# DLRM tower on one Trainium2 core: the sums of two units in one run on TensorE, with a new table of places for the side work

## The reference

```python
e = jnp.stack([tbl_0[ids[:, 0]], ..., tbl_39[ids[:, 39]]], axis=1)   # [512, 40, 32]
iidx, jidx = jnp.triu_indices(40, k=1)
z = jnp.einsum('bpd,pde,bpe->bp', e[:, iidx, :], bilinear_matrices, e[:, jidx, :])   # [512, 780]
h = jnp.concatenate([z, dense_ctx], axis=1)          # [512, 796]
h = jnp.maximum(h @ W_top1 + b_top1, 0.0)            # 796 -> 512
h = jnp.maximum(h @ W_top2 + b_top2, 0.0)            # 512 -> 256
y = h @ W_top3                                       # 256 -> 1
```

## Time and profile before

| | |
|---|---|
| median of 3 runs | 208.48 us (206.97 to 209.49) |
| the profiled execution | 208.05 us, of which the span from first to last instruction 206.0 us |
| TensorE matmul busy | 186.4 us (90% of the span) |
| VectorE busy | 165.7 us (80%) |
| GpSimd busy | 97.7 us (47%) |
| ScalarE busy | 14.7 us (7%) |
| granted TensorE clock, mean | 0.992 |

### The profile page before, as it was taken

The page is one execution under the profiler, slowest core; times in us unless marked ns, Lnnn a source line. Parts: engine busy times, 40 slices in busy tenths (PEclk is TensorE's granted clock), DMA queues, the critical chain, the costliest instruction groups (busy, mean ns, idle before and its releaser), DMA issues.

```text
span 206.0 us, 3187 instructions
## 1 busy us (share of the span) xinstructions
PE 186.4 (90%) x1368; PEld 58.0 (28%) x1368; DVE 165.7 (80%) x168; ACT 14.7 (7%) x23; POOL 97.7 (47%) x101
## 2 busy tenths in 40 slices
PE   0077969999599999999999999999999999999995
PEld 0033313422233432223222222222322222223443
DVE  0399999999999999999987777878989888892500
ACT  2001000010000010100101011101100001001313
POOL 0478777777787777777777777700000000000000
PEclk9999978999999999999999999999999999999999
DMA  5999991001000000010010000000000000000000
GB/s 109 358 402 402 419 397 42 13 16 16 12 14 13 13 13 13 13 18 14 13 16 13 13 13 13 17 5 0 0 5 0 0 0 3 0 0 0 0 0 0
DMA packets 7949, 12.39 MB, mean 60 GB/s; under 512 B 3040, under 2 KB 6000, under 8 KB 7808
## 3 DMA queue, kind: packets, MB, share of 16 engines
q1 hardware_dynamic: 4432, 10.52, 13.7%
q0 software_dynamic: 3072, 1.58, 4.7%
q10 hardware_dynamic: 432, 0.10, 0.3%
HBM read 12.19 MB, written 0.00 MB: 59 GB/s over the span
## 4 chain that ended last, share of the span: by engine, by line
PE 84%; DVE 10%; DMA 4%; issue 1%; SPq 0%; ACT 0%; DVEq 0%
PE y_ps L421 31%; PE z_ps L444 25%; PE t_ps L403 10%; PE t_ps L391 9%; DVE hot L325 4%; DMA table<-hot_tables 4%; PE y_ps L458 3%; DVE low L337 3%; DVE rest L335 3%; PE y_ps L375 2%; PE y_ps L452 2%; PE t_ps L467 1%; DVE prod L357 1%; PE z_ps L436 0%; SPq L254 0%
## 5 line engine op out<-in xcount | busy, mean ns | idle before, releaser
L357 DVE TENSOR_TENSOR prod<-y_ps,xt 128x1024 f32<-128x1024 f32 x110 | 122.2, 1166 | 13.8 <-PE y_ps L421 11.3
L244 POOL DMA_INDIRECT x_rows<-rows,row x96 | 96.7, 1007 | 29.2 <-issue 29.0
L421 PE MATMUL y_ps<-xt,m_sb 32*128 32x512 f32 x420 | 71.0, 649 | 0.0
L444 PE MATMUL z_ps<-prod,sel 128*32 128x512 f32 x420 | 58.3, 604 | 0.0
L421 PEld LDWEIGHTS y_ps<-xt,m_sb 32*128 32x128 f32 x420 | 24.2, 185 | 40.5 <-issue 29.2
L325 DVE TENSOR_SCALAR hot<-hot_id,number 128x2048 bf16<-128x2048 int16 x36 | 25.8, 761 | 8.0 <-DMA hot_id<-hot_ids 7.5
L391 PE MATMUL t_ps<-hot,table 128*32 128x512 bf16 x144 | 15.8, 410 | 17.5 <-DVE low L337 17.5
L403 PE MATMUL t_ps<-z_t,w_sb 128*128 128x512 f32 x40 | 22.2, 642 | 0.0
L444 PEld LDWEIGHTS z_ps<-prod,sel 128*32 128x32 f32 x420 | 8.7, 108 | 41.6 <-issue 27.2
L391 PE MATMUL t_ps<-hot,rest 128*32 128x512 bf16 x144 | 15.6, 406 | 0.0
L391 PE MATMUL t_ps<-hot,low 128*32 128x512 bf16 x144 | 15.5, 402 | 0.0
(11 more groups left out here) (20 smaller groups left out, 32.0 us busy)
## 6 DMA issues: line engine op xcount, KB each, us to landing
hot_id<-hot_ids SPq DMA_DIRECT2D x4, 512.0 KB, 7.2
w_sb<-w SPq DMA_DIRECT2D x1, 1792.0 KB, 18.6
x_rows<-rows,row POOLq DMA_INDIRECT x96, 2.4
table<-hot_tables SPq DMA_DIRECT2D x2, 640.0 KB, 10.6
table<-hot_tables SPq DMA_DIRECT2D x2, 512.0 KB, 8.2
m_sb<-mats SPq DMA_DIRECT2D x1, 640.0 KB
m_sb<-mats SPq DMA_DIRECT2D x1, 576.0 KB
m_sb<-mats SPq DMA_DIRECT2D x1, 512.0 KB
```

The costliest lines, as they stand in the source:

```text
L244: pool.indirect_dma_start(out=x_rows[:, g, c, :], out_offset=None, in_=rows, in_offset=bass.IndirectOffsetOnAxis(ap=row[:, n:n + 1], axis= ...
L357: nc.vector.tensor_tensor(prod[:, k % PROD_UNITS, 2 * half:2 * half + w, :], y_ps[:, 2 * slot:2 * slot + w, :], xt[:, t, :].unsqueeze(1).t ...
L421: last = nc.tensor.matmul(y_ps[:, 2 * slot + s % 2, :], m_sb[rows, k, :], xt[rows, u, :], start=True, stop=True)
L444: last = nc.tensor.matmul(z_ps[s * DIM:(s + 1) * DIM, :], window, prod[:, k % PROD_UNITS, s, :], start=starts, stop=(k >= last_unit(b) - 1 ...
```

## The change: one run of sums behind every second unit

`schedule()` keeps a counter `summed`. Behind the tiles of an odd unit k it now writes all sums that are due by `LAG`, which are two units' (k - 3 and k - 2); behind the tiles of an even unit it writes none. The copy of a block stands behind its last sum as before. The table `AFTER` is another one: which rounds, l1 matmuls and turns stand behind (or ahead of) which unit. Nothing is computed differently, and no instruction is added or taken away. What `AFTER` lists for an even k now stands between the tiles of the two units of a pair, what it lists for an odd k behind the run of sums.

```diff
 AFTER = {
-    "hot": [-1, -1, -1, -1, -1, -1, -1, -1, -1, -1, -1, -1, -1, -1, -1, -1, 0, 1, 1, 1, 1, 2, 2, 3, 3, 3, 7, 7, 8, 8,
-        9, 9, 10, 11, 12, 13],
-    "l1": [26, 27, 28, 29, 30, 31, 32, 33, 34, 35, 36, 37, 42, 44, 45, 46, 47, 47, 48, 49],
-    "turn": [3, 10, 21, 28, 36, 45],
+    "hot": [-1, -1, -1, -1, -1, -1, -1, -1, 0, 0, 0, 0, 0, 0, 1, 1, 1, 1, 2, 3, 3, 4, 4, 5, 6, 6, 6, 7, 7, 8, 8, 10,
+        11, 12, 12, 14],
+    "l1": [24, 26, 28, 30, 31, 32, 34, 36, 40, 42, 42, 43, 44, 44, 46, 47, 48, 50, 52, 52],
+    "turn": [3, 10, 19, 26, 32, 36],
 }
...
     steps = []
+    summed = 0
     for k in range(-1, UNITS + LAG):
         if 0 <= k < UNITS:
             steps.append(("unit", k))
-        if k >= LAG:
-            steps.append(("sum", k - LAG))
-            b, r = divmod(k - LAG, PER_BLOCK)
-            if k - LAG == last_unit(b):
-                steps.append(("z", b))
+
+        while summed <= k - LAG and (k % 2 == 1 or k >= UNITS):
+            steps.append(("sum", summed))
+            if summed == last_unit(summed // PER_BLOCK):
+                steps.append(("z", summed // PER_BLOCK))
+            summed += 1
         for what in ("hot", "l1"):
             steps += [(what, n) for n, after in enumerate(AFTER[what]) if after == k]
     return steps
```

## The result

| | before | changed |
|---|---|---|
| median | 207.87 us (206.97 to 209.49, 4 runs) | 214.28 us (212.41 to 215.04, 4 runs) |
| profiled execution | 208.05 us, span 206.0 | 214.34 us, span 212.5 |
| ratio | | 1.0286, 95% interval 1.019 to 1.0383 |

Slower by 2.9% where 212.6 us was forecast, and inside the range of 208.6 to 215.6. Beside a later pair of kernels the changed one was timed again: 212.54 us (212.14 to 212.87, 4 runs) against 208.05, ratio 1.0206 (1.015 to 1.0262). The forecast was 4.5 us above the kernel before, a ratio of 1.02; by the medians the first set lies 6.4 us above it and the second 4.5.

The account below looks back on a forecast made before the run. VectorE set the pace without side work, TensorE with l1 matmuls. Twenty pairs at 5.37 us plus l1, dense inputs and turn made 113.9 instead of 109.2 us; +4.5 us on 208.05 gave 212.6 us, range 208.6 to 215.6.

Parts of the forecast that it names:

- The loop: Pair's first product, waiting last half, two sums, next tiles: 2.34 + 1.86 + 1.17 = 5.37 us, against VectorE's 4.53.
- Side work between the tiles: One l1 matmul between a pair's tiles costs nothing, two there 0.54 us more; one behind the sums 1.06 more.
- Fewer changes of kind: On TensorE, joined runs save some 0.12 to 0.2 us per change of matmul kind; two sums take 1.86 us.
- rival B: Faster from unit 24 on through saved changes and cheaper l1 matmuls, without loop and turn: 204.2 us, chance 0.07.
- D's wait: The odd unit's second half waits for the product of the even unit's first half, three halves before it.
- The last turn: VectorE's turn, moved from unit 45 to 36, waits for GpSimd's 96th gather; unit 36 not before 136.6 us: 0.7 us.
- The start: Up to unit 14, first product at 75.7 us as before; loss 0, at most 1.3 us from slow TensorE near unit 2.
- sign of being wrong: Prediction wrong if pairs without l1 come at 4.6 us, or the first 75 us differ by more than 2 us.
- 0.55 lost and regained by unit 6: VectorE loses 0.55 us where unit 0's products come ahead of the second table's one-hots, regained by unit 6.
- Rival A: Loop overlapped, pairs without l1 at 4.53 us, but unit 36 still waits until 136.6: 210.2 us, chance 0.13.
- Rival C: Loop as forecast, plus 1.3 us of slow TensorE in the first 35 us and 1.0 of signal: 215 us, chance 0.13.
- 0.05 us of signal in each loop: In the worse case, 0.05 us more of signal in each of 20 loops, 1.0 us in all.

Follow-up runs that it names:

- Experiments 1 and 2: Changed kernel with l1 matmuls moved from between the tiles to behind the sums: 227.76 us; changed kernel with VectorE making an even unit's second product first: 248.84 us.
- the kernels with ten and with eight pairs: Kernel before, l1 matmuls joined between tiles and sums joined only in some pairs: ten, 206.86 us; eight, no l1 run crossing an output-tile change, 205.25 us.
- experiment 3: Changed kernel, but with single sums and the old one-hot places up to unit 13, pairs only from unit 14: 212.73 us, ratio 1.0233.

## Why the prediction was right, point by point

- **The loop, 5.37 us a pair.** Right: 5.35 to 5.37 in the pairs from unit 14 on that have no more than one l1 matmul between the tiles and no wait for a gather (5.41 or 5.42 in those of units 26 and 34), in five kernels. Experiments 1 and 2 lengthen it by an l1 matmul or a product and the pair follows; a count of TensorE's work or of its changes of kind does neither.
- **Side work between the tiles free, behind the sums 1.06, two in the middle 0.54 more.** Right: 5.36 with one in the middle, 6.42 with one behind. The pairs at 42, 44 and 52 with their extras take 6.96, 5.90 and 5.91 us (forecast: 6.97, 5.91 and 5.91), and the 20 pairs 113.2 us, whose sum was forecast at 113.2 without the turn.
- **Fewer changes of kind (rival B).** The saving is what the rows of before gave: two sums 1.86 us. The Trainium skill (TensorEngine Tiling (Array Packing), Tiling Modes) has every change of tiling mode drain TensorE, which speaks for joining. In the changed kernel the time saved reappears as D's wait (0.47 us of pause at 90.48). Only in the kernels with ten and with eight pairs, with the loop hidden, does it reach the end of the kernel.
- **The last turn, 0.7 us.** The mechanism was right and its size a little small: 1.1 us in experiment 3. In the changed kernel's first profile it cost nothing, because VectorE came late for another reason (next point); in its second it cost 0.8 us, the pair of units 34 and 35 taking 6.25 instead of 5.42. The turn there came 3.9 us behind the last gather's issue (132.70 to 136.56), not the 2.4 of the median DMA.
- **The start, 0 to 1.3 us.** This is the term that was mis-sized. Unit 14's first product started at 78.47 us, not at 75.7: 2.7 us, above the bound of 1.3 and above the 2 us that the prediction itself had named as a sign of being wrong. On two other runs with the same first 24 units it started at 76.2 and 76.3, 0.5 late. The windows show the granted clock (column 8) in the stretches 20 to 35 and 50 to 60, first in the changed kernel's first profile, then in its second; the last one is of experiment 3, which has the old start:

```profile
20.00:35.00 15.00, 12.11 (x140) 4.32 (x140) 13.92 (x16) 0.69 (x2) 11.65 (x12) 0.89 0.82 317
50.00:60.00 10.00, 7.48 (x74) 2.08 (x62) 9.97 (x11) 0.60 (x1) 7.86 (x8) 0.83 0.07 12
```

```profile
20.00:35.00 15.00, 10.84 (x150) 3.77 (x144) 14.95 (x18) 0.60 (x1) 11.65 (x12) 1.00 0.79 309
50.00:60.00 10.00, 9.08 (x90) 3.09 (x90) 9.19 (x10) 0.00 (x0) 7.87 (x8) 0.83 0.09 14
```

```profile
50.00:60.00 10.00, 7.36 (x75) 2.32 (x76) 9.97 (x11) 0.00 (x0) 7.86 (x8) 0.83 0.08 13
```

A slow stretch behind TensorE's pause of 2.5 or 2.6 us at 50 us comes in all three. (In the profile of the kernel before, a pause of 2.82 us ends at 53.82, and the clock stays at 1.00.) In experiment 3, with single sums there, it costs nothing: VectorE is busy 9.97 of the 10 us and reaches unit 14 at 75.64. In the changed kernel the tiles of unit 7 and two sums at the low clock lie ahead of unit 8's tiles, and VectorE waits 1.03 us at 61.13 in the first profile and 0.81 at 58.87 in the second. So the prediction had the right mechanism for its upper bound, a slow stretch that makes VectorE wait, but looked for it near unit 2 only. What the paired sums would cost at this place at the full clock no profile shows.

The other 1.3 us or so of the first profile come in the first 35 us. VectorE waits 1.5 us for one-hot rounds between 14 and 18 us, where it waited 0.5 before and 0.2 in the second profile: TensorE's matmuls reach their short duration at 17.1 us, instead of 15.2 and 14.2. And it waits 0.34 us under a low clock between 24 and 27 us, behind a pause of 1.91 us. The kernel before has such a stretch too (granted clock 0.89 from 20 to 35 us) and no wait of VectorE behind it. In both profiles of the changed kernel VectorE also idles 0.70 us ahead of unit 0's first product, which the prediction had as 0.55 lost and regained by unit 6; an idle 0.47 us that the kernel before has ahead of unit 6, at 47.60, is gone instead. That the slow stretches vary from run to run is why two medians of the same kernel differ by 1.7 us, as far as the profiles of one execution each show it. What decides in which run the clock falls stays open; I tried nothing that forces it.
- **By the median** the forecast was 1.7 us low against the first set of runs and met the second (212.54). That it met it to 0.1 us is partly luck: the profiled execution of the second set took 212.87 us, with 0.5 us of late start that the sum had at nothing.
- **Rival A** (210.2) would have needed pairs at 4.53 us; none was found. **Rival C** (215) described the first set best: its 1.3 us of slow stretch in the first 35 us was real, though it had none at 50 us, and its 0.05 us of signal in each loop was not.

## What to carry to other kernels

Before joining steps on an engine, follow the buffer that they share once round: product, release, waiting step, joined run, next producer. The joined run lies in that loop in full, and if the loop is longer than each engine's work the kernel slows down with both engines partly idle. Work that must be done anyway is free where the loop waits (here between the tiles) and costs its full length where it lies in the loop (here behind the sums), so here a join paid where such work stood between the tiles and nothing behind the sums, and lost most where there was none.

## What the runs showed that I had not expected

- TensorE's clock is at risk where the loop makes it pause, but the length of the pause alone doesn't decide it. With pauses of 1.66 us the granted clock was 0.66 over 15 us, a mixture of its 1.2 and 2.4 GHz levels. Behind another pause of 1.66 us, at 116.17, it stayed at 1.00, and on the first chip it fell once in four pauses of 1.11 to 1.66 us between 210 and 232 us (to 0.72 over 223 to 229 us). It also fell in a pair of the same kernel whose pause an l1 matmul had filled but for 0.39 us, at 212.29, with the dense inputs' matmuls behind it. The window:

```profile
209.00:219.00 10.00, 9.61 (x51) 2.17 (x43) 5.22 (x5) 0.38 (x1) 0.00 (x0) 0.83 0.01 2
```

- One chip held every kernel up for over 100 us ahead of unit 0 (329 us for the kernel before); by what, no run shows. At a granted clock of 1.00 the distances between later units were the same there as elsewhere to 0.1 us. Distances inside the profile survived where totals said nothing.
- Between the two profiled executions of the changed kernel, a start 2.3 us later cost only 1.5 us at the end: the wait for the last gather took in the rest.
